# Keys-by-values and numerators as 65- and 66-column matmuls with high and low part side by side

## What is computed

```
qkv = x @ Wqkv + bqkv;  q, k, v = split into heads
q_prime = exp(q @ omega - 0.5*|q|^2);  k_prime = exp(k @ omega - 0.5*|k|^2)
k_sum = sum over rows of k_prime
k_v = einsum('bhnm,bhnd->bhmd', k_prime, v)            # per head 128 x 32
numerator   = einsum('bhnm,bhmd->bhnd', q_prime, k_v)
denominator = einsum('bhnm,bhm->bhn', q_prime, k_sum) + 1e-6
x = layernorm(x + (numerator / denominator) @ Wout + bout)
x = layernorm(x + x @ (Wffn.T + pooled disha))
```

## Time and profile before

| | us |
|---|---|
| median of 3 runs | 2542.88 (2541.21 to 2542.95) |
| the profiled execution's own time | 2542.98 |
| its span in the trace | 2541.2 |

### The profile page before, as it was taken

The page is one execution under the profiler, slowest core; times in us unless marked ns, Lnnn a source line. Parts: engine busy times, 40 slices in busy tenths (PEclk is TensorE's granted clock), DMA queues, the critical chain, the costliest instruction groups (busy, mean ns, idle before and its releaser), DMA issues.

```text
span 2541.2 us, 60675 instructions
## 1 busy us (share of the span) xinstructions
PE 2435.9 (96%) x24584; PEld 1396.0 (55%) x24584; DVE 1797.7 (71%) x3591; ACT 1202.6 (47%) x2049; POOL 469.4 (18%) x522
## 2 busy tenths in 40 slices
PE   5889999999999999999999999999999999998897
PEld 2445555555555555555555555555555555554454
DVE  5556677777677777777777767777767777776776
ACT  2434455445445445545444545444545545544343
POOL 2110211221111221111222121222121122111121
PEclk9999999999999999999999999999999999999999
DMA  5222332332332332233233233233233233231231
GB/s 171 69 59 69 102 89 68 98 93 67 95 89 78 87 98 73 84 89 84 82 102 78 76 93 86 76 102 82 72 102 89 68 98 93 67 95 47 59 97 51
DMA packets 158949, 214.51 MB, mean 84 GB/s; under 512 B 19312, under 2 KB 119760, under 8 KB 154448
## 3 DMA queue, kind: packets, MB, share of 16 engines
q1 hardware_dynamic: 158672, 210.63, 29.7%
HBM read 74.24 MB, written 33.55 MB: 42 GB/s over the span
## 4 chain that ended last, share of the span: by engine, by line
PE 90%; DVE 4%; ACT 2%; issue 1%; SPq 1%; DMA 1%; POOL 0%; DVEq 0%; POOLq 0%; ACTq 0%
PE bank_y L428 25%; PE bank_a L428 23%; PE bank_x L428 13%; PE bank_qf L524 5%; PE bank_kf L472 5%; PE bank_x L554 4%; PE bank_nm L540 2%; PE bank_nm L541 2%; PE bank_nm L542 2%; PE kv_ps L502 2%; PE kv_ps L500 2%; PE kv_ps L497 2%; PE bank_x L441 1%; SPq L347 1%; PE bank_a L441 1%
## 5 line engine op out<-in xcount | busy, mean ns | idle before, releaser
L611 ACT ACTIVATE k_feat<-bank_kf 128x512 f32<-128x512 f32 x512 | 305.6, 597 | 289.5 <-PE bank_kf L472 282.2
L751 DVE TENSOR_TENSOR k_feat_lo<-k_feat 128x512 bf16<-128x512 f32 x512 | 371.6, 731 | 75.2 <-ACT k_feat L611 71.3
L758 DVE TENSOR_TENSOR q_feat_lo<-q_feat 128x512 bf16<-128x512 f32 x512 | 348.9, 688 | 38.4 <-ACT q_feat L620 35.8
L620 ACT ACTIVATE q_feat<-bank_qf 128x512 f32<-128x512 f32 x512 | 305.4, 596 | 145.2 <-PE bank_qf L524 128.9
L869 POOL TENSOR_TENSOR rstd<-mean_var,minus_half 128x1 f32<-128x1 f32 x128 | 71.8, 561 | 1291.8 <-DVE mean_var L824 1291.7
L850 POOL TENSOR_TENSOR xt_lo<-xt_f,xt_hi 128x512 f16<-128x512 f32 x132 | 163.6, 1267 | 461.9 <-DVE xt_hi L655 445.3
L856 POOL TENSOR_TENSOR rows<-rows,bias_out 128x512 f32<-128x512 f32 x128 | 176.1, 1377 | 301.1 <-DMA rows<-x 294.8
L497 PE MATMUL kv_ps<-v_hi,k_feat 128*128 128x33 f16 x2048 | 208.9, 178 | 9.8 <-DVE k_feat_lo L751 9.5
L472 PE MATMUL bank_kf<-omega_s,stack_k 98*128 98x128 f16 x2048 | 200.7, 220 | 16.0 <-DMA stack_k<-half_norm 8.5
L497 PEld LDWEIGHTS kv_ps<-v_hi,k_feat 128*128 128x128 bf16 x2048 | 176.3, 97 | 59.2 <-DVE k_feat_lo L751 17.3
L502 PE MATMUL kv_ps<-v_hi,k_feat_lo 128*128 128x33 f16 x2048 | 206.7, 177 | 0.0
(11 more groups left out here) (159 smaller groups left out, 5341.4 us busy)
## 6 DMA issues: line engine op xcount, KB each, us to landing
xt_f<-xt SPq DMA_DIRECT2D x33, 1024.0 KB, 5.3
stack_k<-t_hi_k SPq DMA_DIRECT2D x256, 128.0 KB, 2.4
rows<-x SPq DMA_DIRECT2D x128, 256.0 KB, 2.9
out<-rows SPq DMA_DIRECT2D x128, 256.0 KB, 2.1
stack_q<-t_hi_q SPq DMA_DIRECT2D x240, 128.0 KB, 2.4
stack_k<-t_lo_k SPq DMA_DIRECT2D x128, 128.0 KB, 2.4
stack_q<-t_lo_q SPq DMA_DIRECT2D x120, 128.0 KB, 2.4
stack_k<-t_hi_q SPq DMA_DIRECT2D x16, 128.0 KB, 2.8
```

The lines of the kernel that those rows point to most:

```text
L611: nc.scalar.activation(k_feat[:, i % 2, :], bank_kf[:, :], ACT.Exp, scale=1.0 / WS).then_inc(S["k_exp"], 1)
L620: nc.scalar.activation(q_feat[:, 2 * pair:2 * pair + 2, :], bank_qf[:, :].rearrange("p (e n) -> p e n", e=2), ACT.Exp, scale=1.0 / WS).the ...
L751: v.tensor_tensor(k_feat_lo[:, u, :], k_feat[:, u, :], k_feat_hi[:, u, :], ALU.subtract).then_inc(S["kfl"], 1)
L758: v.tensor_tensor(q_feat_lo[:, at, :], q_feat[:, at, :], q_feat_hi[:, at, :], ALU.subtract).then_inc(S["qfl"], 1)
```

## The change

- v_hi and v_lo become one array v_both: per head 33 columns of high part and ones, then 32 of low part (WV = 65). kv_hi and kv_lo become views of kv_both (33 and 33, WN = 66).
- KV: high features by v_both in one matmul of 65 columns, into 65 columns of kv_ps, then low features by the first 33 columns into the first 33. A PSUM bank has 512 columns, so that 7 of its 8 heads (WIDE) are wide, and the eighth keeps its three matmuls into 33 columns.
- NM: likewise with 66 and 33 columns. High and low sum now lie beside each other in the bank. ScalarE copies the seven low sums into nm_l (33 zeros stand for the eighth), VectorE adds the bank's high sums and nm_l into nm_f, and den and the product read nm_f. PE's next NM waits for that sum (nm_sum) where it waited for normed.
- KFIN goes in halves, one for each kv_ps bank, KFIN0 and KFIN1, with an addition of the low columns and one for the eighth head; kfin counts halves, and NM0 and NM1, KV0 and KV2 wait for their own half.
- ORDER: KFIN in halves ahead of VP0 and behind YT3; NM0 ahead of QP2. VectorE takes NM with a lag of 1 and AT with none.
- The query-only end: alone now holds for the chunk of ORDER_LAST too; odd NM go to bank_kf, QP stay in bank_x; ORDER_LAST and ORDER_Q are rewritten, with NM in pairs.

```diff
+WV = W1 + DH
+WN = W1 + W1
+WIDE = 7
...
-QF3 KP3 KV13' QF4 KF15' QP1. KV14' QF5 KN QF6 QP1 FF2'. QF7 KV15' FF2' KFIN' VP0. YT3' VP0 QP2. NM0 Z2'
+QF3 KP3 KV13' QF4 KF15' QP1. KV14' QF5 KN QF6 QP1 FF2'. QF7 KV15' FF2' KFIN0' VP0. YT3' KFIN1' VP0 NM0 QP2. Z2'
...
-KP0. KF4' KP0 KV3' KF5' KP1. KFIN' KV4' KF6' KP1 KV5' KF7' KP2. KV6' KF8' KP2 KV7' KF9' KP3. KV8' KF10'
+KP0. KF4' KP0 KV3' KF5' KP1. KV4' KF6' KP1 KV5' KF7' KP2. KV6' KF8' KP2 KV7' KF9' KP3. KV8' KF10'
...
-AT3' KF12' KV11' WO3'. QF0 KF13' KV12' WO3' YT2' QP1. KF14' QF1 KV13' QP1 KF15' KV14' FF2'. QF2 YT3' FF2' QF3
-KV15' KFIN' QP2. QF4 QP2 QF5 Z2' QF6 QP3. QF7 QP3 NM0 FF3'. NM1 FF3' AT0 NM2 QF8 WO0. NM3 Z3' WO0 AT1 QF9 WO1.
-YT0 QF10 WO1 QF11 FF0. QF12 FF0 QF13 YT1 QF14 QF15 QN Z0 FF1. NM4 FF1 NM5
+KF12' AT3' KV11' WO3'. QF0 KF13' KV12' WO3' YT2' QP1. KF14' QF1 KV13' QP1 KF15' KV14' FF2'. QF2 YT3' FF2' QF3
+KV15' KFIN0' KFIN1' QP2. QF4 QP2 QF5 Z2' QF6 FF3'. QF7 FF3' QP3. NM0 NM1 QP3 NM2 AT0 Z3' NM3 QF8 WO0. QF9 WO0
+AT1 QF10 YT0 QF11 WO1. QF12 WO1 QF13 FF0. QF14 FF0 QF15 YT1 Z0 FF1. QN NM4 FF1 NM5
...
-QP0. AT2' NM6' QP0 NM7' QF0 WO2'. AT3' QF1 WO2' Z1' QF2 WO3'. YT2' QF3 WO3' QF4 QP1. QF5 QP1 QF6 FF2'. QF7 YT3'
-FF2' QP2. NM0 QP2 NM1 FF3'. Z2' AT0 NM2 FF3' NM3 QF8 WO0. AT1 QF9 WO0 QF10 QP3. QF11 QP3 YT0 Z3' QF12 WO1. QF13
-WO1 QF14 FF0. QF15 FF0 QN YT1 FF1. NM4 Z0 FF1 NM5
+QP0. AT2' NM6' NM7' QP0 QF0 WO2'. QF1 WO2' AT3' Z1' QF2 QP1. YT2' QF3 QP1 QF4 WO3'. QF5 WO3' QF6 FF2'. QF7 YT3'
+FF2' QP2. NM0 NM1 QP2 FF3'. AT0 NM2 NM3 FF3' QF8 WO0. Z2' QF9 WO0 AT1 QF10 QP3. YT0 QF11 QP3 Z3' QF12 WO1. QF13
+WO1 QF14 FF0. QF15 YT1 FF0 QN NM4 NM5 Z0 FF1. FF1
...
-DVE_LAGS = {"AT": 1, "FF": 1, "KF": 1, "KFIN": 1, "KP": 1, "QF": 1, "QN": 2, "QP": 1, "VP": 1, "WO": 1, "YT": 1}
+DVE_LAGS = {"AT": 0, "NM": 1, "FF": 1, "KF": 1, "KFIN": 1, "KP": 1, "QF": 1, "QN": 2, "QP": 1, "VP": 1, "WO": 1, "YT": 1}
...
-BEHIND_US = {"KP": 1.4, "VP": 0.8, "QP": 1.4, "KF": 0.8, "QF": 0.8, "AT": 0.8, "YT": 0.8, "QN": 1.0, "KFIN": 1.0, "FF": 1.2}
+BEHIND_US = {"KP": 1.4, "VP": 0.8, "QP": 1.4, "KF": 0.8, "QF": 0.8, "AT": 0.8, "YT": 0.8, "QN": 1.0, "KFIN": 1.0, "FF": 1.2,
+             "NM": 0.6}
...
-        v_hi = sb("v_hi", [P, TPC, H, W1], F16)
-        v_lo = sb("v_lo", [P, TPC, H, DH], F16)
-        kv_hi = sb("kv_hi", [P, H, W1], BF16)
-        kv_lo = sb("kv_lo", [P, H, W1], BF16)
+        v_both = sb("v_both", [P, TPC, H, WV], F16)
+        kv_both = sb("kv_both", [P, H, WN], BF16)
+        kv_hi, kv_lo = kv_both[:, :, 0:W1], kv_both[:, :, W1:WN]
...
+        nm_f, nm_l = (sb(f"nm_{s}", [P, 8, W1], F32) for s in "fl")
...
-            if alone(b, c) and kind in ("AT", "YT", "QP"):
-                return kv_ps[0] if kind != "QP" else bank_x if i % 2 else bank_kf
+            if alone(b, c) and kind in ("AT", "YT"):
+                return kv_ps[0]
...
+        def bank_nm_of(b, c, i):
+
+            return bank_kf if alone(b, c) and i % 2 else bank_nm
+
+        def units(bank):
+
+            return bank[:, 0:(WIDE + 8) * W1].rearrange("p (u w) -> p u w", w=W1)
...
-                return 4 if alone(b, c) else 2
+                return 4 if c else 2
...
-            return CPB * b + c - CPB > LAST_Q
+            return CPB * b + c >= CPB * B
...
-                    if i == 0 and c == 0:
-                        wait(pe, "kfin", b)
+                    if i in (0, HPG // 2) and c == 0:
+                        wait(pe, "kfin", 2 * b - 1 + i // 2)
...
-                        at = W1 * (h % 8)
+                        at = WV * (h % 8)
+                        width = WV if h % 8 < WIDE else W1
...
-                        nc.tensor.matmul(o[:, at:at + W1], hi, v_hi[:, t, h, :],
+                        nc.tensor.matmul(o[:, at:at + width], hi, v_both[:, t, h, 0:width],
                                          start=c == 0 and t == 0 and h % 8 == 0, stop=False,
                                          skip_group_check=True)
-                        nc.tensor.matmul(o[:, at:at + DH], hi, v_lo[:, t, h, :], start=False, stop=False,
-                                         skip_group_check=True)
-                        last = nc.tensor.matmul(o[:, at:at + W1], lo, v_hi[:, t, h, :], start=False,
+                        if width == W1:
+                            nc.tensor.matmul(o[:, at:at + DH], hi, v_both[:, t, h, W1:WV], start=False,
+                                             stop=False, skip_group_check=True)
+                        last = nc.tensor.matmul(o[:, at:at + W1], lo, v_both[:, t, h, 0:W1], start=False,
                                                 stop=end, skip_group_check=True)
...
-                    if i == 0:
-                        wait(pe, "kfin", b)
-                    wait(pe, "normed", 8 * j + i)
+                    if i < 2:
+                        wait(pe, "kfin", 2 * b - 1 + i)
+                    bank = bank_nm_of(b, c, i)
+                    if bank is bank_kf:
+                        wait(pe, "k_exp", 16 * B * CPB)
+                    wait(pe, "nm_sum", 8 * j + (max(i - 1, 0) if alone(b, c) else i))
                     for hl in range(8):
                         h = 8 * u + hl
                         hh = G * (h % HPG) + h // HPG
                         pos = slice(P * (t % 2), P * (t % 2 + 1))
-                        o = bank_nm[:, W1 * hl:W1 * (hl + 1)]
-                        nc.tensor.matmul(o, q_feat_hi[:, hh, pos], kv_hi[:, h, :], start=True, stop=False)
-                        nc.tensor.matmul(o, q_feat_hi[:, hh, pos], kv_lo[:, h, :], start=False, stop=False)
-                        last = nc.tensor.matmul(o, q_feat_lo[:, hh, pos], kv_hi[:, h, :], start=False,
-                                                stop=True)
+                        at = WN * hl
+                        width = WN if hl < WIDE else W1
+                        nc.tensor.matmul(bank[:, at:at + width], q_feat_hi[:, hh, pos], kv_both[:, h, 0:width],
+                                         start=True, stop=False, skip_group_check=True)
+                        if width == W1:
+                            nc.tensor.matmul(bank[:, at:at + W1], q_feat_hi[:, hh, pos], kv_lo[:, h, :],
+                                             start=False, stop=False, skip_group_check=True)
+                        last = nc.tensor.matmul(bank[:, at:at + W1], q_feat_lo[:, hh, pos], kv_hi[:, h, :],
+                                                start=False, stop=True, skip_group_check=True)
                     last.then_inc(S["nm_done"], 1)
...
-                            wait(act, "kfin", b)
+                            wait(act, "kfin", 2 * b)
...
-                    nc.scalar.activation(v_hi[:, i, :, 0:DH],
+                    nc.scalar.activation(v_both[:, i, :, 0:DH],
...
+                elif kind == "NM":
+                    m = 8 * j + i + 1
+                    wait(act, "nm_done", m)
+                    wait(act, "nm_sum", m - 1)
+                    nc.scalar.activation(nm_l[:, 0:WIDE, :], units(bank_nm_of(b, c, i))[:, 1::2, :],
+                                         ACT.Copy).then_inc(S["nm_low"], 1)
...
+            v.memset(nm_l[:, WIDE, :], 0.0).then_inc(S["dve_const"], 1)
+            v.memset(v_both[:, :, :, DH:W1], 1.0).then_inc(S["dve_const"], 1)
...
-                    v.tensor_tensor(v_lo[:, i, :, :],
+                    v.tensor_tensor(v_both[:, i, :, W1:WV],
                                     bank_of(b, c, kind, i)[:, :].rearrange("p (h d) -> p h d", d=DH),
-                                    v_hi[:, i, :, 0:DH], ALU.subtract).then_inc(S["v_lo_done"], 1)
+                                    v_both[:, i, :, 0:DH], ALU.subtract).then_inc(S["v_lo_done"], 1)
...
-                    for uu in range(2):
-                        src = heads(kv_ps[uu])
-                        dst = kv_f[:, 8 * uu:8 * uu + 8, :]
-                        v.tensor_tensor(dst[:, :, 0:DH],
-                                        bias_v16[:, 256 * uu:256 * (uu + 1)].rearrange("p (h d) -> p h d", d=DH),
-                                        src[:, :, DH:W1].to_broadcast([P, 8, DH]),
-                                        ALU.mult).then_inc(S["fin_a"], 1)
-                        v.tensor_copy(dst[:, :, DH:W1], src[:, :, DH:W1]).then_inc(S["fin_a"], 1)
-                    done = b + c // CPB
-                    wait(dve, "fin_a", 4 * done + 4)
-                    for uu in range(2):
-                        dst = kv_f[:, 8 * uu:8 * uu + 8, 0:DH]
-                        v.tensor_tensor(dst, heads(kv_ps[uu])[:, :, 0:DH], dst, ALU.add).then_inc(S["fin_b"], 1)
-                    wait(dve, "fin_b", 2 * done + 2)
-                    v.tensor_copy(kv_hi[:, :, :], kv_f[:, :, :]).then_inc(S["fin_c"], 1)
-                    wait(dve, "fin_c", done + 1)
-                    v.tensor_tensor(kv_lo[:, :, :], kv_f[:, :, :], kv_hi[:, :, :],
+                    n = 2 * (b + c // CPB) + i + 1
+                    own = slice(8 * i, 8 * i + 8)
```

(26 more changed lines are left out.)

15 lines of the change are left out of this document (6 added, 9 removed).

## The result

| | before | after |
|---|---|---|
| median, us | 2542.05 (2537.45 to 2542.95) | 2516.9 (2513.97 to 2518.6) |
| span of the profiled execution, us | 2541.2 | 2514.4 |

The account below looks back on a forecast made before the run. TensorE was taken as the bound, busy 96% of the span. Gains 65.9 + 14 - 11 + 2.5 + 4 = 75 us off 2543 gave 2468 us (forecast 2455 to 2482, chance 0.68), range 2453 to 2500.

Parts of the forecast that it names:

- Part 1: Keys-by-values and numerator matmuls: three per head become two, 30 ns at 66 columns; saves 2.35 us a slot, 65.9 us.
- (a): Rival on the wide matmuls: width costs more, 35.7 ns each, total about 2488 us; chance 0.09.
- (b): Rival on the wide matmuls: width is free since the weight load sets the pace, total 2452 us; chance 0.05.
- (e): Rival on the wide matmuls: nothing happens, a 66-column pair costs two floors, 51 ns; total 2536 us; chance 0.02.
- Part 2: ScalarE copy and VectorE sum per numerator piece: covered by matmuls, with 0.4 us a slot of waits, 11 us lost.
- (c): Rival on the queues: 1.2 us and more a slot of in-order waiting, total 2490 to 2538 us; chance 0.12.
- Part 2, the division: VectorE's division reading numerators from SBUF instead of PSUM: no change in time, 688 against 682 ns for 512 elements.
- Part 4: NM0 ahead of QP2 fills its wait, 6 us over 21 slots; end sum in halves, 8 us over seven slots.
- Part 5: Key-only slots at the beginning: keys-by-values save 4.7 us of issue, half counted, 2.5 us (0 to 4.7).
- Part 6: Query-only end: shorter numerators, reordering and 2.5 us of cover against added VectorE work; 4 us net gain (-6 to +10).

Follow-up runs that it names:

- e19: Whole change with better places in ordinary slots and the end, plus one 264-element VectorE addition behind each division that nobody waits for: 2522.4 us, 0.9943.
- e13: Keys-by-values half alone, with the end sum's first half ahead of KV15 and NM5 behind the first half of the next slot's KP0: 2491.3 us, 0.9807.
- e12: Keys-by-values half alone, plus one 264-element VectorE addition ahead of each of the 256 divisions, its result not needed: 2599.3 us, 1.0242.

## Why the prediction was wrong

The profiled executions differ by 26.8 us, where the sum had 75. By its terms, over the 27 slots that the slot starts cover (the forecast counted 28; the 28th lies in the beginning):

| term | forecast | measured |
|---|---|---|
| 1, wide matmuls, 2.35 a slot | 65.9 | 63.2 (2.34 a slot) |
| 4, NM0 ahead of QP2, halves | 14 | 12.2 (0.655 - 0.021 - 0.183 a slot) |
| 2, new waits in the steady part | -11 | -36.6 (1.36 a slot) |
| 5, the beginning | 2.5 | -0.6 |
| 6, the end | 4 | -11.3 |

**Part 1** was right within a nanosecond: 30 for 65 and 66 columns, a head of the piece shown 55.7 (forecast 55.5). Of the rivals (a), (b) and (e) fall. The line through three points of the trace beat the page: the Trainium skill, TensorE: Matmul & The Clock Gate, section Back-to-back issue gap, would have had 45 ns by that estimate.

**Part 2** was right in the added steps' durations: the sum 426 ns (forecast 432), the copy 364 (350), and VectorE 80% busy over the steady part. Windows of 1200 to 2200, before and after:

```profile
1200.00:2200.00 1000.00, 991.89 (x10135) 572.45 (x10134) 727.92 (x1463) 494.66 (x845) 190.03 (x211) 1.00 0.31 87
```

```profile
1200.00:2200.00 1000.00, 984.84 (x8862) 554.13 (x8861) 801.96 (x1625) 534.18 (x972) 198.59 (x221) 1.00 0.32 88
```

The step that failed is the sentence "covered by the 0.3 to 1.5 us of matmuls between numerator pieces", and the 0.4 us a slot put on it, where 1.36 came. It asked how far apart the numerator pieces are on TensorE. It should have asked, for each piece, what VectorE does just ahead of it and what TensorE has left to issue until somebody needs the result. At AT3 there were only the four matmuls of an output projection, and the division stood behind a step that itself waited for ScalarE. That one place was half of the new waiting (0.68 of 1.36 us a slot), and the swap removed it with no other work taken away: this half is shown. Most of the other half stands at NM5, KV5, AT2, QF13 and QP3. That VectorE's greater load is behind it is likely and not shown: e19 passes on a third of 3.5 us, and the change adds about as much (3.4 by the forecast), but the two measured prices, 0.6 for the place and some 1.1 for the load, come to more than the 1.36, and with the best places found the numerators still cost 0.72 us of waits. How places, load and stretched steps divide it stays open. Rival (c), "1.2 us and more a slot of in-order waiting", 2490 to 2538, is what came, and it had a chance of 0.12. The prediction's own count gave a hint, in hindsight: with 1.7 us of waits a slot at 73% of VectorE, 0.4 more at 80% was the hopeful reading. No run shows a rule for it.

**Part 2, the division** "reads its numerators from SBUF ... so nothing" was mis-sized as well: den went from 162 to 244 ns on average and the product from 424 to 466 (the last section says why). With 8 pieces a slot that is 8 x 0.124 = 1.0 us more of VectorE in each. The Trainium skill's VectorE: DVE Perf Modes, section The TRN2 errata, pointed the other way, to less.

**Part 4** was right: QP2's wait is gone. In an ordinary slot of the kernel after, as the earlier trace rows:

```profile
1339.30 1.03 PE L437 MATMUL bank_a<-wqkv_hi,xt_lo 128*128 128x512 f16 x4
...
1340.16 0.19 PE L555 MATMUL bank_nm<-kv_both,q_feat 128*128 128x66 bf16 x1
...
1340.63 0.59 PE L437 MATMUL bank_x<-xt_hi,wqkv_hi 128*128 128x512 f16 x2
```

NM0 starts 0.86 us after the four matmuls, the time they take to issue, and QP2 right behind it. In a slot with an end sum NM0 waits 0.8 us for half 0, where the forecast's times had 0.56 (1133.04 to 1133.6), and half 0 takes 2.25 us (forecast 2.2); e13 shows that the wait goes when the half is asked for earlier. QP2's 1.9 us become 0.1 there, so 1.0 is won, the forecast had 1.1. The experiment that put NM0 back gave 0.35 us a slot, the forecast 0.5.

**Part 5**: the beginning gave nothing. In keys-by-values alone the same five slots take 260.5 us, one less than before. In the experiments, which leave the orders of the key-only slots alone, they take anything from 255.6 to 263.3 us, so a term of 2.5 can't be read here.

**Part 6** had the wrong sign, and lies outside its bounds of -6 to +10. It weighed the 3.4 us of VectorE a chunk, and held the 2.5 us of cover for enough. The part runs by the length of chains, and the chain copy, sum, division grew by some 0.9 us (an estimate from 0.36 and 0.43 and two hops) per numerator piece that is waited for. That the sum and the stretched steps of the division are the loss is shown together (slots 33 to 36 take 214.7 us without them, 228.0 with them, 216.9 before), and that the new order with its second bank helps by 12 us against the old one. Keys-by-values alone has no such loss.

**The numbers.** The forecast had 0.68 and was 49 us too low; the upper end of 2500 took in only part of (c). "Faster" was right.

## What to carry to other kernels

Work given to an engine that isn't the bound is not free when the engines run in fixed orders. For each place where the bounding engine takes that work's result, write down what stands ahead of it in the helper's queue, and what the bounding engine still has to issue: the shortest cover counts, not the spacing on average. With VectorE at 81% in the steady part, a third of extra work that nobody waits for reached the slot. When such an edit disappoints, list the waits by piece and move the producer in its queue before giving the edit up: swapping two neighbours gave 19.5 us, moving the consumer nothing.

## What the hardware showed that I had not expected

VectorE's small steps on numerators in SBUF are sometimes stretched to over 1 us. Groups by form: the division in the kernel after; then den in the kernel before and in the one with keys-by-values and the added sum (e12), which both read it from PSUM:

```profile
L826 DVE TENSOR_TENSOR attn<-nm_f,den 128x256 f32<-128x256 f32 x256 | 119.3, 466 | 8.8
...
L819 DVE TENSOR_SCALAR den<-nm_f 128x8 f32<-128x8 f32 x256 | 62.4, 244 | 8.8
```

```profile
L789 DVE TENSOR_SCALAR den<-bank_nm 128x8 f32<-128x8 f32 x256 | 41.5, 162 | 170.8 <-PE bank_nm L542 170.6
```

```profile
L806 DVE TENSOR_SCALAR den<-bank_nm 128x8 f32<-128x8 f32 x256 | 42.6, 166 | 8.8
```

The median of den in the kernel after is 172 ns, but 41 of the 256 are long, up to 1251, and of the products 14, up to 1310 (median 424). All 55 begin while one GpSimd operation runs, the addition of the output bias, which reads two operands from SBUF, and end a fixed time behind its end: den after 25 to 32 ns, the product after 280 to 286. All 14 products that begin in such an addition are long. Steps that begin before it are not, nor are the 56 sums (one operand in the bank) and the 13 reciprocals that begin in it. A scene in the end, where it reached TensorE:

```profile
2360.74 2.49 POOL L886 TENSOR_TENSOR rows<-rows,bias_out 128x512 f32<-128x512 f32 x2
2360.95 1.08 DVE L819 TENSOR_SCALAR den<-nm_f 128x8 f32<-128x8 f32 x1
2362.30 1.21 DVE L826 TENSOR_TENSOR attn<-nm_f,den 128x256 f32<-128x256 f32 x1
...
2365.04 0.66 PE L572 MATMUL kv_ps<-ident,attn 128*128 128x128 f32 x4 [1.98 <-DVE attn L826]
```

In the kernel before, 85 den and 114 product steps overlap GpSimd's work and none is long (162 and 424 ns on average); they read PSUM. In all, the stretching costs 18.3 + 10.5 us of VectorE in 2514.

The kernel before had the effect already, on the low part of the key features, which takes both operands from SBUF: its mean stands 43 ns above that of q_feat_lo in the earlier trace rows, with 34 of 512 long, up to 1647 ns, all begun while a GpSimd addition or subtraction of two SBUF operands runs.

```profile
L751 DVE TENSOR_TENSOR k_feat_lo<-k_feat 128x512 bf16<-128x512 f32 x512 | 371.6, 731 | 75.2 <-ACT k_feat L611 71.3 <-PE kv_ps L502 0.6
```

So the price of moving numerators to SBUF could have been asked from this row. The Trainium skill, SBUF — State Buffer, section Who interferes with whom, states that a VectorE instruction with two SBUF inputs, or in one of its two-port modes, and a GpSimd instruction that reads SBUF exclude each other for a whole instruction, while one with at most one SBUF input outside those modes is not disturbed. The rows of the product, the sum and k_feat_lo agree. The den step has one SBUF input, as the undisturbed reciprocal has; it fits the statement only if it runs in a two-port mode, which no row here shows. How much of the missing 49 us this took wasn't measured apart: neither the bias addition on another engine nor a wide division that reads its numerators from PSUM was tried. Keys-by-values alone divides out of the bank; that this is part of its advantage is only argued.
